# Sixteen turns of a state-space stage, written out on every engine instead of looped

## The reference

```python
def _mamba(x, in_w, cw, cb, xpw, dtw, dtb, A_log, Dp, ow):
    xz = x @ in_w
    u, z = jnp.split(xz, 2, axis=-1)                      # 512 channels each
    up = jnp.pad(u, ((0, 0), (D_CONV - 1, 0), (0, 0)))
    u = jax.nn.silu(cb + sum((up[:, k:k + L, :] * cw[:, k] for k in range(D_CONV))))
    proj = u @ xpw
    dt, Bm, Cm = proj[..., :16], proj[..., 16:32], proj[..., 32:]
    delta = jax.nn.softplus(dt @ dtw + dtb)
    A = -jnp.exp(A_log)                                   # 512 x 16 states
    def step(h, inp):                                     # over 512 tokens
        d_t, b_t, c_t, u_t = inp
        h = jnp.exp(d_t[..., None] * A) * h + (d_t * u_t)[..., None] * b_t[:, None, :]
        return (h, jnp.einsum('bdn,bn->bd', h, c_t))
    ...
    return (y + u * Dp) * jax.nn.silu(z) @ ow
for i in range(in_proj_w.shape[0]):                       # 4 layers
    x = _layer_norm(_mamba(x, ...) + x, ln_w[i], ln_b[i])
```

## Time and profile before

| | before |
|---|---|
| time, median of 3 | 4595.32 us (4593.82 to 4601.95) |
| profiled execution | 4597.94 us, its span 4596.1 us |
| DVE busy | 3349.5 us, 73% of the span |
| PE busy | 3209.3 us, 70% |
| POOL busy | 2260.4 us, 49% |
| ACT busy | 1798.0 us, 39% |
| mean granted TensorE clock | 0.813 |

### The profile page before, as it was taken

One profiled execution on the slowest core, in us unless ns is written; L12 is line 12 of the kernel. 1 busy time (PEld: TensorE's weight loads), 2 busy tenths in 40 slices (PEclk: granted clock), 3 DMA queues, 4 the chain that ended last, 5 costly groups with the idle time before them and its releaser, 6 DMA issues. The chain is left out here.

```text
span 4596.1 us, 53330 instructions
## 1 busy us (share of the span) xinstructions
PE 3209.3 (70%) x16134; PEld 1764.4 (38%) x16134; DVE 3349.5 (73%) x4084; ACT 1798.0 (39%) x2796; POOL 2260.4 (49%) x905
## 2 busy tenths in 40 slices
PE   6767888856658837777877778777887778548422
PEld 2326777743436512333333333333332333224211
DVE  2445666675401129999999999999999999966597
ACT  2233333313211126445554455445554455314232
POOL 0001111122120027788888888888888888732222
PEclk8766777768679968889988899888998889879765
DMA  1000000000212231112111121111211111110100
GB/s 36 0 0 6 0 0 0 0 5 17 79 55 99 74 94 46 63 56 84 58 64 62 52 78 67 55 62 55 84 66 51 57 64 56 63 39 0 36 0 18
DMA packets 85634, 207.16 MB, mean 45 GB/s; under 512 B 12619, under 2 KB 43554, under 8 KB 84802
## 3 DMA queue, kind: packets, MB, share of 16 engines
q1 hardware_dynamic: 79682, 197.78, 12.7%
q0 software_dynamic: 3072, 6.00, 0.7%
q10 hardware_dynamic: 2816, 2.62, 0.2%
HBM read 194.09 MB, written 14.68 MB: 45 GB/s over the span
## 5 line engine op out<-in xcount | busy, mean ns | idle before, releaser
L1894 POOL TENSOR_TENSOR mb_h<-mb_h,mb_BC 128x1024 f32<-128x1024 f32 x512 | 1681.0, 3283 | 338.2 <-DVE mb_h L2079 338.2
L2180 PE MATMUL mb_y<-mb_h,ident 128*128 128x512 f32 x2048 | 1059.9, 660 | 413.9 <-POOL mb_h L1894 413.4
L2079 DVE TENSOR_TENSOR_SCAN mb_h<-mb_dA,mb_bx 128x1024 f32<-128x1024 f32 x512 | 1170.5, 2286 | 57.0
L1976 ACT ACTIVATE mb_dA<-mb_delta,mb_A 128x511 f32 (+1 forms) x1024 | 668.2, 712 | 750.3 <-DVE mb_h L2079 748.8
L2180 PEld LDWEIGHTS mb_y<-mb_h,ident 128*128 128x128 f32 x2048 | 405.6, 208 | 1026.6 <-POOL mb_h L1894 594.8
L2074 DVE TENSOR_TENSOR mb_bx<-mb_du,mb_BC 128x1024 f32<-128x1024 f32 x512 | 756.4, 1477 | 25.1 <-POOL mb_du L1876 4.9
L1633 DVE TENSOR_TENSOR me_h<-me_s,me_p 128x320 f32<-128x320 f32 x64 | 31.3, 488 | 290.9 <-ACT me_s L1611 290.9
L254 PE MATMUL mb_p<-mb_xT,mb_in_w 128*128 128x512 f32 x512 | 237.6, 598 | 4.2 <-DMA mb_in_w<-in_L_attn_in_proj_w 4.2
L254 PE MATMUL mb_p<-mb_upad,mb_convd 128*128 128x512 f32 x512 | 230.5, 593 | 1.1 <-ACT mb_upad L1930 0.7
L707 POOL COPY rs_vs<-rw_v 128x256 f32 x16 | 9.8, 611 | 444.7 <-PE rs_p L969 336.9
L2173 PE MATMUL mb_y<-mb_u,mb_diagD 128*128 128x512 f32 x128 | 94.1, 902 | 162.3 <-DVE mb_yg L2049 162.3
(11 more groups left out here) (431 smaller groups left out, 5788.5 us busy)
## 6 DMA issues: line engine op xcount, KB each, us to landing
mb_BC<-mamba_BC SPq DMA_DIRECT2D x128, 1024.0 KB, 5.2
me_W<-in_L_ffn_W SPq DMA_DIRECT2D x24, 1024.0 KB, 8.6
mb_in_w<-in_L_attn_in_proj_w SPq DMA_DIRECT2D x4, 1024.0 KB, 7.8
mb_convd<-in_mamba_taps SPq DMA_DIRECT2D x4, 1024.0 KB, 9.8
expert_rows<-me_zero SPq DMA_DIRECT2D x1, 2560.0 KB, 10.2
x<-in_x SPq DMA_DIRECT2D x1, 2048.0 KB, 8.4
me_xe<-expert_rows SPq DMA_DIRECT2D x8, 256.0 KB, 10.6
expert_results<-me_oe ACTq DMA_DIRECT2D x8, 256.0 KB, 7.7
```

Of the source, the lines that this page charges most:

```text
L1894: tt(hk, hk, BC[e % 2][:, 1, :, :], ALU.mult).then_inc(*pos(f"hc{k}{part}"))
L1976: i = av(dA[k % 2][:, c, s, 1:], delta[:, ds(it % 2, 1), mc, 1:].rearrange("p o t -> p (o t)"), ACT.Exp, scale=A[:, ds(first(it) + mc, 1), ...
L2079: nc.vector.tensor_tensor_scan(flat(h[k % NBUF][:, c, :, :]), flat(dA[k % 2][:, c, :, :]), flat(full(bx)), 0.0, ALU.mult, ALU.add).then_in ...
L2180: i = mm(ybank[half * CU + c][:, :], m.ident[:, :], h[k % NBUF][:, c, s, :], start=False, stop=e == SPLIT - 1 and s == SU - 1)
```

## The change

The `Fori` of each of the five engines in this stage becomes a Python `range`. The program then holds the body of every turn one after the other, and turn numbers are constants: counts, buffers and rows are known when the program is built. No computing instruction and no transfer is added or dropped.

```diff
@@ block.sync
-                with sp.Fori(0, NL6 - 1) as l:
+                for l in range(NL6 - 1):
                     body(B * l, tail_layer=l)
                     body(B * l + 1)
                     body(B * l + 2, next_layer=l + 1)
@@ block.gpsimd
-                with po.Fori(1, TURNS - 1) as it:
+                for it in range(1, TURNS - 1):
                     body(it)
@@ block.scalar
-                with a.Fori(1, TURNS - 2) as it:
+                for it in range(1, TURNS - 2):
                     body(it)
@@ block.vector
-                with v.Fori(1, TURNS - 1) as it:
+                for it in range(1, TURNS - 1):
                     body(it)
@@ block.tensor
-                with t.Fori(1, TURNS - 2) as it:
+                for it in range(1, TURNS - 2):
                     body(it)
```

## The result

The changed kernel takes 4748.57 us (median of 4, 4740.07 to 4751.62), against 4597.79 us for the kernel before (4 runs): ratio 1.0325, 95% interval 1.0307 to 1.0343. That is 151 us more, where 146 were forecast (a time of 4742 us). The profiled execution took 4740.07 us, its span 4738.2 us.

The account below looks back on a forecast made before the run. DVE (VectorE) was taken as the bound. Fourteen middle turns at 156.63 instead of 146.06 us gave +148.0, less 0.2 and 2.2, so +146 us and a timed 4742 us; range 4710 to 4765.

Parts of the forecast that it names:

- The bound: State-space stage: DVE is never kept waiting by PE, ACT, POOL or a load, so only its own stream sets time.
- Back edges at nothing: Loop branches between turns: 13 back edges on DVE at 0.01 us each, nothing; other engines' edges also nothing.
- Shorter waits between `bx` and scan: Each `bx`-to-scan start on DVE: 1.27 us instead of 1.36, a gain of 2.9 us a turn.
- The race lost at odd steps: First part of odd steps: POOL's product starts ahead of `bx`, which takes 3.42 us; 128 places instead of 16.
- The sum: Middle turns built from straight-code stretches: 156.63 us against 146.06, times 14, less turn-end corrections, +146 us.
- Step 1's place: First part of step 1, counted among the 8 odd-step places a turn where `bx` loses to POOL.
- races won: Rival: DVE wins the odd-step races in middle turns; 139.35 us a turn, -94 us, 4501 us; chance 0.05.
- The price of a place: Cost on DVE of one lost race at an odd step: stretched pair 5.77 against 3.61 us, 2.16 us.
- The rule of a full lock: Read port shared by DVE and POOL locked for a whole instruction: late `bx` 3.55 us, against 3.42 in the row.

Follow-up runs that it names:

- the repaired kernels: Changed kernel, all engines straight, with VectorE's wait for PE held (4491.81 us) or swapped in source with the scan's wait (4490.24 us), so `bx` carries the scan's wait.

## Why the prediction was right

- *The bound.* DVE waited on a semaphore for no other engine in the middle turns, before or after. Right, with one thing to add: what POOL costs DVE shows in no view of waits, since it lies inside the duration of `bx`.
- *Back edges at nothing.* 3.38 us across the branch, 3.37 without, 3.37 after. With DVE's loop put back and the others straight the time is that of the kernel before, so the other engines' edges were worth nothing too.
- *Shorter waits between `bx` and scan.* 2841.33 - 2840.06 = 1.27 us after the change, as foreseen.
- *The race lost at odd steps.* The core of it, shown from both sides: `bx` started 0.07 us earlier, or POOL 0.10 us later, takes away the loss, and more lost places cost in proportion. The reason it could be read ahead of time is that turns 0 and 15 already ran in the new form in the old trace.
- *The sum.* 156.61 us a turn against 156.63, stage +145.6 against +145.6; the median moved 151 us, 5 more than that. The profiled executions differ by 142 us with the same +145.6 in the stage, so parts that the change does not touch vary by some us from one execution to the next, and the changed kernel's four times spread from 4740 to 4752. The missing 5 us lie within that; no trace shows where.
- *What was off.* Step 1's place in turns 2 to 15 was counted among the races. With DVE's wait repaired its `bx` still takes 3.29 us: in straight code it is a backlog of POOL, wherever the wait stands. That did not touch the sum, which took the row as it stood, but it touches the rival "races won": seven places a turn can be won, not eight, and a turn takes 140.86 us, where it was put at 139.35. The price of a place was under-sized in turn: 2.16 us left out 0.09 us that the wait in front adds, and the runs show 2.25 to 2.30. The rival was put at 4501 us and the repaired kernels came out at 4490 to 4492; that the two lie close is in part luck, since turns 0 and 15, which the rival left alone, gained too.
- *The rule of a full lock*, which the prediction takes from the Trainium skill, page "SBUF — State Buffer", section "Who interferes with whom", would have had a late `bx` at 3.55 us. All 113 lost races show 3.40 to 3.43: the measurement decides, and POOL lets go about 0.13 us before the end that the profile gives it.

## What to carry to other kernels

Where two instructions that cannot run side by side are released by the same event, as `bx` and POOL's product here, who starts first is decided by hundredths of a microsecond, and so by which of an instruction's waits it carries itself. A change that "only" makes waits constant can move that. Let the instruction on the bounding engine carry the wait that comes last, and read it off the instruction order, not off the source. When a change turns a loop into straight code, look for turns that were straight already: their trace is the trace of the new kernel.

## What was not expected

The best versions take 4485 to 4490 us, 2.3 to 2.4% under the kernel with loops, from two swapped lines beside DVE's unrolling. With the same instructions the order of two waits is worth 4748.57 - 4490.24 = 258 us, more than twice the 108 us that the unrolling gains once the waits are right (4598.36 - 4490.24). And a slower POOL made the kernel faster: started 0.1 us later at each of 512 products, it gave 242 to 250 us back (4498.85 against 4740.35 and 4748.57).
